# Spreading v over partitions: 10 transfers a tile in place of 16

## The chip, the cores and the metric

The kernel runs on one core of a Trainium2 chip. The metric is the device time of one execution in microseconds (us), the median of several runs. Engines are named as in the profile: PE is TensorE, DVE is VectorE, ACT is ScalarE, POOL is GpSimd, SP is SyncE, which here only issues DMA transfers.

## What is computed

The input x is 2048 tokens by 128 features. A stack of six layers (windowed attention with 16 heads of 64, window 32, then a gated feed-forward part) is run over the normalised input, half of its result is added to x, a Mamba block follows, and the same stack is run once more. What matters here is the attention:

```python
def local_attention(q, k, v):
    b, h, n, d = q.shape
    w = WINDOW                       # 32
    nw = n // w
    bq = q.reshape(b, h, nw, w, d)
    bk = k.reshape(b, h, nw, w, d)
    bv = v.reshape(b, h, nw, w, d)
    def look(t):                     # each window sees itself and the window before
        p = jnp.pad(t, ((0, 0), (0, 0), (1, 0), (0, 0), (0, 0)))
        return jnp.concatenate([p[:, :, :nw], p[:, :, 1:]], axis=3)
    bk2, bv2 = (look(bk), look(bv))
    ...
    out = jnp.einsum('bhwij,bhwje->bhwie', attn, bv2)
for i in range(DEPTH):               # 6
    x = attn_layer(shift_tokens(x), ...) + x
    x = ffn_layer(shift_tokens(x), ...) + x
```

Each window of 32 queries is multiplied with 64 rows of v: the 32 of the window before and its own 32.

## The kernel before

A stack works through N = 96 tiles (16 tiles of 128 tokens, 6 layers), and runs twice. A loop over steps s issues, on each engine, one instruction group of several tiles in an order written out by hand; tile n is projected near step n+18 to n+20 and leaves the attention at step n+23. The engines meet through semaphores alone.

On PE a step is, in this order: scores_high, k_project, out_project (L379), q_transpose (L235), values (L357), k_transpose (L235), in one step of four the feed-forward products (L418 to L420), q_project and v_project (L191 to L193), scores_low (L318 and L296), in one step of four each ffn_centre (L397) and ffn_down (L484), p_transpose (L235) and ffn_variance (L411). The layout of the steps repeats every four tiles, called a cycle here.

The path of v: v_project(n) writes a PSUM slot that q_transpose, v_project and p_transpose take in turns. v_evacuate(n) on ACT (L703) copies it to VT[n % 2], 128 rows (tokens) by 1024 values, and PE's p_transpose(n-1) waits for that copy (L333), because it writes the same slot. SP's spread_values(n) waits for the copy (L1367) and then for values(n-2) (L1371), and issues the transfers that lay v out in V2[n % 2] as four windows of 64 rows for two halves of the heads: destination rows 0 to 63 for one half of the columns, 64 to 127 for the other. Window w holds rows 32w-32 to 32w+31 of the tile; window 0 takes its first 32 rows from the tile before. Each is an SBUF to SBUF DMA of 32 rows of 512 f32 values, that is 64 KB; there are 2 x 4 x 2 = 16 a tile (L1376 and L1378, in turns).

Two waits hold the transfers of a tile n-1 complete: PE's values(n-1) at L344, and ACT's v_evacuate(n) at L700, since the buffer VT[(n-1) % 2] is read by the transfers of two tiles and overwritten by the copy after next. So the copy of tile n starts after all transfers of tile n-1 have landed, and the transfers of tile n start after the copy. ACT works in order: behind v_evacuate stand restore_tables, inverse_norms (L688, L693), carry_evacuate, ffn_square, ffn_rsqrt and p_evacuate (L756).

Of the kernel before, what the change touches and what calls it, by code (L numbers as in the profile page):

```python
# [31 lines left out]
def build(nc, xT, consts, wqkv, wo, w1, w2, lpar, qks, mpar, in_w, xp_w, dt_w, out_w, out):  # L32
    ctx = ExitStack()
    with ctx:
# [3 lines left out]
        def sem(name):  # L38
            return ctx.enter_context(nc.semaphore("s_" + name))
# [27 lines left out]
        def take(n):  # L67
            top[0] += n
            assert top[0] <= 34400, top[0]
            return ARENA[:, top[0] - n:top[0]]  # L70
# [21 lines left out]
        QN, KN, QT, VT = ([take(1024) for _ in range(2)] for _ in range(4))  # L92
# [38 lines left out]
        v2_in = [sem(f"v2_in{i}") for i in range(2)]  # L131
# [34 lines left out]
        def tensor_stack(pe, r):  # L166
            n0, c0, l0 = N * r, 4 * NL * r, NL * r

            def after_tile(eng, sem, n):
                if n >= 0:  # L170
                    eng.wait_ge(sem, n0 + min(n, N - 1) + 1)

            def after_chunk(eng, sem, c):
                if c >= 0:
                    eng.wait_ge(sem, c0 + min(c, N // 4 - 1) + 1)
# [164 lines left out]
            def values(n):  # L340
                if not 0 <= n < N:
                    return
                pe.wait_ge(PT_ev, n0 + n + 1)
                pe.wait_ge(v2_in[n % 2], 256 * ((n0 + n) // 2 + 1))  # L344
                s = n + 22
                after_tile(pe, sub_done, s - 21)
                if s < RAMP or s >= N:
                    after_chunk(pe, f_h[1], (s - 24) // 4 - 1)
                    after_tile(pe, oT_ev, s - 23)
                pt = PTS.rearrange("p (h w x) -> p h w x", h=8, w=4)  # L350
                v2 = V2[n % 2].rearrange("p (w h d) -> p w h d", w=4, h=8)
                for m in range(4):
                    for win in range(4):
                        for side in range(2):
                            hp, col = 2 * m + side, 32 * win
                            out = PS[64 * side:64 * side + 64, 3, 256 * m:256 * m + 256]
                            last = nc.tensor.matmul(  # L357
                                out.rearrange("p (a q) -> p a q", a=2)[:, :, col:col + 32], v2[:, win, hp, :],
                                pt[:, hp, win, :], start=True, stop=True, skip_group_check=True)
                last.then_inc(pv_done, 1)  # L360
# [136 lines left out]
            for s in range(STEPS):  # L497
                scores_high(s - 21)
                k_project(s - 19)
                out_project(s - 23)  # L500
                q_transpose(s - 20)
                values(s - 22)
                k_transpose(s - 20)
                ffn_up0(s - 24)
                ffn_up1(s - 24)
                ffn_up2(s - 24)
                q_project(s - 18)
                v_project(s - 20)
                scores_low(s - 20)
                carry(s - 19)  # L510
                ffn_centre(s - 23)
                ffn_down(s - 24)
                p_transpose(s - 21)
                ffn_variance(s - 23)
# [95 lines left out]
        def scalar_stack(act, r):  # L610
            n0, c0, l0 = N * r, 4 * NL * r, NL * r
# [83 lines left out]
            def v_evacuate(n):  # L695
                if not 0 <= n < N:
                    return
                act.wait_ge(v_done, n0 + n + 1)
                if n:
                    act.wait_ge(v2_in[(n - 1) % 2], 256 * ((n0 + n - 1) // 2 + 1))  # L700
                if n == 1:
                    act.wait_ge(zero_set, r + 1)
                act.activation(VT[n % 2], PS[:, 2, :], ACT.Copy).then_inc(v_ev, 1)  # L703
# [133 lines left out]
            for s in range(STEPS):  # L837
                if s == 19 + 4:
                    high_input(3)
                ffn_high(s - 23)  # L840
                split_k(s - 18)
                exponentials(s - 20)
                q_evacuate(s - 19)
                o_evacuate(s - 21)
                k_evacuate(s - 19)
                gelu0(s - 23)
                gelu1(s - 23)
                gelu2(s - 23)
                q_square(s - 17)
                v_evacuate(s - 19)  # L850
                restore_tables(s - 23)
                inverse_norms(s - 18)
                carry_evacuate(s - 18)
                split_input(s - 24)
                ffn_square(s - 22)
                ffn_rsqrt(s - 22)
                p_evacuate(s - 20)
                k_square(s - 17)
                split_v(s - 19)
                split_q(s - 17)  # L860
# [487 lines left out]
        def sync_stack(sp, r):  # L1348
            n0, c0, l0 = N * r, 4 * NL * r, NL * r

            def load_projection(l):
                for g in range(3):
                    s = slice(1024 * g, 1024 * g + 1024)
                    sp.dma_start(WS[:, s], wqkv[l, :, s]).then_inc(ws_in[g], 16)

            def load_weights(l):
                sp.dma_start(WO[l % 2], wo[l]).then_inc(wo_in[l % 2], 16)
                sp.dma_start(W2[l % 2], w2[l]).then_inc(wo_in[l % 2], 16)

            def load_up(l):  # L1360
                sp.dma_start(W1, w1[l]).then_inc(w1_in, 16)

            def spread_values(n):
                if not 0 <= n < N:
                    return
                v2 = V2[n % 2].rearrange("p (w c) -> p w c", w=4)
                sp.wait_ge(v_ev, n0 + n + 1)  # L1367
                if n == 0:
                    sp.wait_ge(zero_set, r + 1)
                if n >= 2:  # L1370
                    sp.wait_ge(pv_done, n0 + n - 1)  # L1371
                for par in range(2):
                    c = slice(512 * par, 512 * par + 512)
                    for win in range(4):
                        src = VT[n % 2][32 * win:32 * win + 32, c]
                        sp.dma_start(v2[64 * par + 32:64 * par + 64, win, :], src).then_inc(v2_in[n % 2], 16)  # L1376
                        src = VT[n % 2][32 * win - 32:32 * win, c] if win else VT[(n - 1) % 2][96:128, c]
                        sp.dma_start(v2[64 * par:64 * par + 32, win, :], src).then_inc(v2_in[n % 2], 16)  # L1378

            load_projection(0)  # L1380
            load_up(0)
            if r == 0:
                for a, b in ((C[:, 512:1664], consts[:, 512:1664]), (LP, lpar), (QKS, qks), (MP, mpar)):
                    sp.dma_start(a[:, :], b).then_inc(const_in, 16)
            for l in range(2):
                load_weights(l)
            for n in range(N):
                spread_values(n)
                l, T = divmod(n, NT)
                if l + 1 < NL and T == 2:  # L1390
                    for g in range(3):
                        sp.wait_ge(w_lo[g], l0 + l + 1)
                    load_projection(l + 1)
                if l + 1 < NL and T == 12:
                    sp.wait_ge(w1_lo, l0 + l + 1)
                    load_up(l + 1)
                if 1 <= l < NL - 1 and T == 13:
                    sp.wait_ge(f_y, c0 + 4 * l)
                    sp.wait_ge(wo_done, n0 + NT * l)
                    load_weights(l + 1)  # L1400
# [139 lines left out]
```

## Time and profile before

| | |
|---|---|
| median of 3 runs | 3566.99 us (3557.14 to 3574.47) |
| profiled execution | 3554.87 us |
| its span | 3553.0 us |
| granted clock of PE, mean | 0.977 |
| PE busy | 3213.8 us, 90% |
| DVE, ACT, POOL busy | 79%, 71%, 69% |
| DMA q1 (all that SP issues) | 237.59 MB, 27.7% of 16 engines |
| transfers of v | 3072 of 64.0 KB |

The page shows the two stacks (PE at nine tenths) and between them, in a sixth of the span, the Mamba block, in which no v is spread. Times in the views are from the start of the span. An issue row of SP (written SPq) is the time that the queue's instruction took, not the transfer; what was released by a transfer's landing is written as a wait on "DMA ARENA<-ARENA". All large buffers lie in one array, so most rows say ARENA, and the line number tells which step it is.

### The profile page before, as it was taken

Reading aid. Unit: us, or ns where it says so; the run is one execution under the profiler, and the core shown is the slowest. Engines: PE = TensorE matmul, PEld = TensorE weight load, DVE = VectorE, ACT = ScalarE, POOL = GpSimd, SP = SyncE. Lnnn points to the kernel's source line nnn. Section 1 sums busy time; section 2 is a strip of 40 time slices with the busy share of each in tenths; the row PEclk is TensorE's granted clock in tenths of the full one; section 3 lists DMA queues with packets and bytes.
Section 4 is the critical chain, followed back from the end, with each engine's and each line's share of the span. In section 5 each row is a group of like instructions: output and inputs, shape, how many; then the busy total and the mean of one; then the engine's idle time right before and its main releaser. Section 6 shows DMA issues by size and latency. Waiting matters only on the chain. (4 is left out here: it accounts for less than half of the span.)

```text
span 3553.0 us, 121372 instructions
## 1 busy us (share of the span) xinstructions
PE 3213.8 (90%) x51488; PEld 2519.5 (71%) x51488; DVE 2810.5 (79%) x3179; ACT 2508.1 (71%) x3154; POOL 2454.6 (69%) x1241
## 2 busy tenths in 40 slices
PE   6999999999999999986776799999999999999997
PEld 4777777777777777772222677777778778777775
DVE  6787888888788788765886778888888888788884
ACT  4777777777777777766665567777777777777764
POOL 5676776777777677640998667777767668667662
PEclk8999999999999999998999899999999999999999
DMA  3333333233333333221000223333323323323222
GB/s 96 88 75 81 71 82 86 68 79 85 70 79 83 72 75 70 65 61 45 0 0 0 74 68 70 85 73 73 90 66 82 87 66 83 81 68 81 66 63 54
DMA packets 160308, 245.36 MB, mean 69 GB/s; under 512 B 50781, under 2 KB 52638, under 8 KB 159646
## 3 DMA queue, kind: packets, MB, share of 16 engines
q1 hardware_dynamic: 159774, 237.59, 27.7%
q8 instruction: 415, 6.80, 0.8%
q14 instruction: 119, 0.97, 0.1%
HBM read 35.01 MB, written 1.05 MB: 10 GB/s over the span
## 5 line engine op out<-in xcount | busy, mean ns | idle before, releaser
L1269 POOL TENSOR_TENSOR ARENA<-ARENA,RN 128x1024 f32<-128x1024 f32 x192 | 365.3, 1903 | 550.8 <-ACT RN L693 550.7
L235 PE MATMUL PS<-C,ARENA 128*128 128x128 f32 x4608 | 618.5, 278 | 112.5 <-ACT ARENA L703 88.4
L235 PEld LDWEIGHTS PS<-C,ARENA 128*128 128x128 f32 x4608 | 513.0, 141 | 199.1 <-issue 164.0
L1261 POOL TENSOR_TENSOR ARENA<-ARENA 128x1024 f32<-128x1024 f32 x192 | 468.5, 2440 | 264.7 <-DVE ARENA L1002 263.7
L191 PE MATMUL PS<-WL,XH 128*128 128x512 f32 x1152 | 491.1, 426 | 42.4 <-DVE ARENA L987 18.0
L756 ACT ACTIVATE ARENA<-PS 64x1024 f32<-64x1024 f32 x384 | 390.1, 1016 | 111.6 <-PE PS L235 108.2
L1255 POOL TENSOR_TENSOR ARENA<-ARENA 128x1024 f32<-128x1024 f32 x192 | 457.5, 2383 | 8.2 <-DVE ARENA L987 8.1
L357 PE MATMUL PS<-ARENA 128*64 128x64 f32 x12288 | 405.6, 225 | 58.9 <-DVE ARENA L1040 35.4
L193 PE MATMUL PS<-WH,XH 128*128 128x512 f32 x1152 | 457.2, 397 | 0.0
L192 PE MATMUL PS<-WH,XL 128*128 128x512 f32 x1152 | 455.3, 395 | 0.0
L357 PEld LDWEIGHTS PS<-ARENA 128*64 128x64 f32 x12288 | 380.9, 139 | 93.5 <-issue 92.9
L1283 POOL TENSOR_TENSOR ARENA<-ARENA,RI 128x1024 f32<-128x1024 f32 x192 | 365.8, 1905 | 69.6 <-DVE RI L1051 62.9
L980 DVE TENSOR_TENSOR ARENA<-PS,TAB 128x1024 f32<-128x1024 f32 x192 | 235.1, 1225 | 224.5 <-ACT ARENA L675 224.5
L379 PEld LDWEIGHTS PS<-ARENA 128*128 128x128 f32 x3072 | 373.0, 192 | 19.8 <-ACT ARENA L765 2.5
L1032 DVE TENSOR_REDUCE MX<-PS 128x16 f32<-128x1024 f32 x192 | 234.8, 1223 | 189.7 <-PE PS L296 186.5
L379 PE MATMUL PS<-ARENA 128*128 128x128 f32 x3072 | 375.1, 275 | 2.9 <-ACT ARENA L765 2.2
L1277 POOL TENSOR_TENSOR ARENA<-ARENA,RN 128x1024 f32<-128x1024 f32 x192 | 374.6, 1951 | 0.0
L296 PEld LDWEIGHTS PS<-ARENA 64*32 64x32 f32 x24576 | 295.2, 105 | 70.8 <-issue 60.2
L296 PE MATMUL PS<-ARENA 64*32 64x64 f32 x24576 | 329.7, 224 | 0.2 <-issue 0.2
L703 ACT ACTIVATE ARENA<-PS 128x1024 f32<-128x1024 f32 x192 | 196.5, 1024 | 179.7 <-DMA ARENA<-ARENA 142.9
L765 ACT ACTIVATE ARENA<-PS 128x1024 f32<-128x1024 f32 x192 | 197.0, 1026 | 144.5 <-PE PS L357 144.5
L191 PEld LDWEIGHTS PS<-WL,XH 128*128 128x128 f32 x1152 | 218.8, 190 | 103.2 <-issue 40.2
(137 smaller groups left out, 6492.6 us busy)
## 6 DMA issues: line engine op xcount, KB each, us to landing
ARENA<-ARENA SPq DMA_DIRECT2D x3072, 64.0 KB
ARENA<-in_wqkv SPq DMA_DIRECT2D x36, 512.0 KB, 4.9
ARENA<-in_wo SPq DMA_DIRECT2D x12, 512.0 KB, 4.0
ARENA<-in_w SPq DMA_DIRECT2D x12, 341.0 KB, 3.5
ARENA<-in_w SPq DMA_DIRECT2D x12, 192.0 KB, 4.8
X<-in_xT SPq DMA_DIRECT2D x4, 256.0 KB, 5.2
out<-X SPq DMA_DIRECT2D x1, 1024.0 KB, 3.9
QKS<-in_qks SPq DMA_DIRECT2D x1, 768.0 KB, 8.4
```

The lines of the kernel that those rows point to most:

```text
L191: nc.tensor.matmul(o, XH[:, x], WL[:, s], start=True, stop=False)
L192: nc.tensor.matmul(o, XL[:, x], WH[:, s], start=False, stop=False)
L193: last = nc.tensor.matmul(o, XH[:, x], WH[:, s], start=False, stop=True)
L235: last = nc.tensor.transpose(PS[:, slot, 128 * j:128 * j + 128], src[:, 128 * j:128 * j + 128], ident)
L296: last = nc.tensor.matmul(PS[32 * win:32 * win + 32, 3, c:c + 64], q[a:b, hp, 32 * win:32 * win + 32], kt[a:b, hp, 32 * win:32 * win + 64] ...
L357: last = nc.tensor.matmul(out.rearrange("p (a q) -> p a q", a=2)[:, :, col:col + 32], v2[:, win, hp, :], pt[:, hp, win, :], start=True, st ...
L379: last = nc.tensor.matmul(PSB[:, 2, 0:128], w[:, 128 * j:128 * j + 128], OTS[:, 128 * j:128 * j + 128], start=j == 0, stop=j == 7)
L756: last = act.activation(blocks[a:b, :, par, :], PS[a:b, 2, :].rearrange("p (b q) -> p b q", q=32), ACT.Copy)
L1255: nc.gpsimd.tensor_tensor(QN[n % 2], QN[n % 2], T2, ALU.add).then_inc(q_add, 1)
L1261: nc.gpsimd.tensor_tensor(KN[n % 2], KN[n % 2], T2, ALU.add).then_inc(k_add, 1)
L1277: nc.gpsimd.tensor_tensor(a, a, bc(RN[:, n % 2, 16:32], 64), ALU.mult).then_inc(k_nrm, 1)
L1283: nc.gpsimd.tensor_tensor(heads(P), heads(P), bc(RI[:, n % 2, :], 64), ALU.mult).then_inc(p_nrm, 1)
```

## The change

The transfers whose source rows adjoin are joined: for windows 1 to 3 one transfer of 64 rows takes the place of two of 32, and window 0 keeps two of 32 (one from the tile before, one from its own). A tile has 2 x (2 + 3) = 10 transfers, 4 of 64 KB and 6 of 128 KB, with the same bytes to the same places. Each adds 16 to its semaphore, so the two waits count 160 a tile in place of 256.

```diff
@@ values (PE)
-                pe.wait_ge(v2_in[n % 2], 256 * ((n0 + n) // 2 + 1))
+                pe.wait_ge(v2_in[n % 2], 160 * ((n0 + n) // 2 + 1))
@@ v_evacuate (ACT)
-                    act.wait_ge(v2_in[(n - 1) % 2], 256 * ((n0 + n - 1) // 2 + 1))
+                    act.wait_ge(v2_in[(n - 1) % 2], 160 * ((n0 + n - 1) // 2 + 1))
@@ spread_values (SP)
+                last = VT[(n - 1) % 2][96:128, :]
                 for par in range(2):
-                    c = slice(512 * par, 512 * par + 512)
-                    for win in range(4):
-                        src = VT[n % 2][32 * win:32 * win + 32, c]
-                        sp.dma_start(v2[64 * par + 32:64 * par + 64, win, :], src).then_inc(v2_in[n % 2], 16)
-                        src = VT[n % 2][32 * win - 32:32 * win, c] if win else VT[(n - 1) % 2][96:128, c]
-                        sp.dma_start(v2[64 * par:64 * par + 32, win, :], src).then_inc(v2_in[n % 2], 16)
+                    a, c = 64 * par, slice(512 * par, 512 * par + 512)
+                    sp.dma_start(v2[a:a + 32, 0, :], last[:, c]).then_inc(v2_in[n % 2], 16)
+                    sp.dma_start(v2[a + 32:a + 64, 0, :], VT[n % 2][0:32, c]).then_inc(v2_in[n % 2], 16)
+                    for win in range(1, 4):
+                        src = VT[n % 2][32 * win - 32:32 * win + 32, c]
+                        sp.dma_start(v2[a:a + 64, win, :], src).then_inc(v2_in[n % 2], 16)
```

## Rows read from the trace of the kernel before

**Rows 1.** Busy time of all engines in one stretch of 255 us, four cycles:

```profile
core 0: us, PE busy (x) PEld busy (x) DVE busy (x) ACT busy (x) POOL busy (x), PEclk, DMA share, GB/s
567.00:822.00 255.00, 243.95 (x4247) 200.92 (x4245) 210.49 (x242) 190.56 (x237) 183.27 (x92) 0.99 0.33 79
```

**Rows 2.** PE's waits over the span: us in total, times, longest:

```profile
PE PS L235 <- ACT ARENA L703: 88.4, 103, 2.8
...
PE PS L357 <- DVE ARENA L1040: 35.4, 45, 1.3
```

**Rows 3.** ACT's waits over the span, those of v_evacuate:

```profile
ACT ARENA L703 <- DMA ARENA<-ARENA: 142.9, 88, 3.7
...
ACT ARENA L703 <- PE PS L193: 36.8, 104, 1.0
```

**Rows 4.** The line of v_evacuate: count, ns min/median/max, first and last start:

```profile
L703 ACT ACTIVATE ARENA<-PS x192: 1023/1023/1027, 56.0 to 3501.9; 128x1024 f32<-128x1024 f32 x192
```

**Rows 5.** ACT in order of time, seven of the 192 copies of v (L703):

```profile
702.53 1.02 ACT L703 ACTIVATE ARENA<-PS 128x1024 f32<-128x1024 f32 x1 [2.44 <-DMA ARENA<-ARENA]
...
716.91 1.02 ACT L703 ACTIVATE ARENA<-PS 128x1024 f32<-128x1024 f32 x1 [0.35 <-PE PS L193]
...
736.29 1.02 ACT L703 ACTIVATE ARENA<-PS 128x1024 f32<-128x1024 f32 x1 [0.33 <-PE PS L193]
...
752.21 1.03 ACT L703 ACTIVATE ARENA<-PS 128x1024 f32<-128x1024 f32 x1 [0.35 <-PE PS L193]
...
815.84 1.02 ACT L703 ACTIVATE ARENA<-PS 128x1024 f32<-128x1024 f32 x1 [0.35 <-PE PS L193]
829.03 1.02 ACT L703 ACTIVATE ARENA<-PS 128x1024 f32<-128x1024 f32 x1 [0.44 <-DMA ARENA<-ARENA]
844.24 1.02 ACT L703 ACTIVATE ARENA<-PS 128x1024 f32<-128x1024 f32 x1 [2.45 <-DMA ARENA<-ARENA]
```

**Rows 6.** SP's queue in order of time: the transfers of one tile:

```profile
703.58 0.51 SPq L1376 DMA_DIRECT2D ARENA<-ARENA  x1
704.13 0.59 SPq L1378 DMA_DIRECT2D ARENA<-ARENA  x1
704.76 0.59 SPq L1376 DMA_DIRECT2D ARENA<-ARENA  x1
...
707.30 1.45 SPq L1376 DMA_DIRECT2D ARENA<-ARENA  x1
...
713.87 0.59 SPq L1378 DMA_DIRECT2D ARENA<-ARENA  x1
```

**Rows 7.** The chain that ended last, two landings of a tile's last transfer:

```profile
3215.93 3.90 DMA ARENA<-ARENA
...
3413.11 2.04 DMA ARENA<-ARENA
```

**Rows 8.** PE in order of time: transposes after v_evacuate, and values:

```profile
703.70 1.94 PE L235 MATMUL PS<-C,ARENA 128*128 128x128 f32 x8 [2.31 <-ACT ARENA L703]
...
726.23 2.08 PE L357 MATMUL PS<-ARENA 128*64 128x64 f32 x64 [0.38 <-DVE ARENA L1040]
...
789.87 2.08 PE L357 MATMUL PS<-ARENA 128*64 128x64 f32 x64 [1.04 <-DVE ARENA L1040]
...
817.01 1.07 PE L235 MATMUL PS<-C,ARENA 128*128 128x128 f32 x8 [0.21 <-ACT ARENA L703]
```

**Rows 9.** Busy time in stretches of 2 us around the stall at 703:

```profile
702.00:704.00 2.00, 0.30 (x2) 0.33 (x3) 1.60 (x2) 1.35 (x3) 0.00 (x0) 0.84 0.00 0
704.00:706.00 2.00, 2.00 (x41) 1.67 (x39) 0.00 (x0) 0.74 (x3) 1.81 (x1) 0.50 0.28 66
706.00:708.00 2.00, 2.00 (x59) 1.62 (x40) 1.15 (x1) 1.71 (x2) 2.00 (x2) 0.81 0.50 114
```

**Rows 10.** Issue time of a weights load, 128 rows, 512 KB each:

```profile
L1354 SPq DMA_DIRECT2D ARENA<-in_wqkv x36: 328/455/601, 3.1 to 3035.7; - x36
```

**Rows 11.** DVE in order of time, row_max of one step:

```profile
721.68 1.23 DVE L1032 TENSOR_REDUCE MX<-PS 128x16 f32<-128x1024 f32 x1 [1.61 <-PE PS L296]
```

## The prediction

> **What bounds the kernel now.** I read the stretches by engine first. In a stack PE is busy 244 of 255 us, DVE 211, POOL 184 [rows 1]. So PE sets the pace of most steps, and all that a change off PE can win is its idle time, about 11 us in 255, plus what those stalls cost behind them. The list of PE's waits says whose it is: the largest entry is p_transpose (L235) held by the copy of v (L703), 88.4 us in 103 waits; next comes values (L357) held by DVE's subtraction, 35.4 us [rows 2]. The copy of v in turn waits 142.9 us, in 88 of its 192 executions, for transfers to land, and in the other 104 only for the end of v_project, 0.35 us a time [rows 3, 5].
>
> The loop behind it can be timed in one tile. The copy starts at 702.53 and takes 1.02; the first transfer is issued at 703.58, the sixteenth at 713.87, that is 10.29 us for fifteen spacings, fourteen or so of them 0.633 us and one longer because an issue took 1.45 [rows 5, 6]. The last transfer lands 2.04 to 3.90 us after its issue began, mostly near the lower end [rows 7]. Then the next copy may start. The sum is 1.05 + 10.3 + 2.1 = 13.5 us at the least, 15.3 with a late landing.
>
> Against this stands the length of a step when only PE limits it. The starts of the copies give four kinds of step in a cycle. Into the copy at 736.29 (feed-forward products) it is 19.38 us, into that at 752.21 (ffn_down) 15.92, into 829.03, almost without a wait for DMA, 13.19. After a step as short as that the following one is long, 15.21, with 2.45 of waiting [rows 5]. Over all 192 starts [rows 4] the two short kinds last 14.23 us (48 of them) and 14.34 (46) on the mean, and never under 13.12. So the transfer loop binds two steps of four, at 14.3 against 13.15 us, and the two long ones hide it.
>
> **The change, part by part.** *Removed:* six issues a tile. *Added:* nothing on any engine; no wait is new, the two counts only follow the number of transfers. The bytes stay at 1 MB a tile. *Moved:* nothing passes another instruction on SP; the weights loads behind a tile's transfers are issued about 4 us earlier, which nobody waits for.
>
> Nine spacings are left. At the present spacing they are 9 x 0.633 = 5.7 us, with a long issue up to 6.8. The loop becomes 1.05 + 5.7 to 6.8 + 2.1 to 3.9 = 8.9 to 11.8 us. This lies under 13.15 by 1.3 us at the worst, so the loop no longer binds any step.
>
> The price of a 64-row issue is the unknown. The nearest rows are the 32-row issue at 0.59 us [rows 6] and the weights load with 128 rows and eight times the bytes, at 0.455 us [rows 10]. Both say that rows do not cost issue time, so I take 0.6; the ends are 0.45 and, if the cost followed the rows, 1.18. Even at 1.18 (spacing about 1.22) the ten take 4 x 0.633 + 5 x 1.22 = 8.6 us to the last start, and the loop 11.8 with an early landing, 13.6 with a late one: most of the gain would stay.
>
> The moving of the bytes is the other unknown. While 32-row transfers are issued back to back, the DMA engines are busy 0.50 of the time, at 114 GB/s [rows 9]. With 64 rows in the same spacing that doubles to about 1.0 for three transfers running, then falls again. One transfer's own time may so grow by some 0.2 to 0.3 us, which I put on the landing; it is inside the margin above.
>
> A rule of the Trainium skill speaks against the change here (page "SBUF — State Buffer", section "Door 1: The DMA port swizzle"): rows p and p+32 lie on the same port, so 64 rows reach no more ports than 32 do and move no faster in total. By its figures a transfer of 128 KB over eight ports would take about 0.6 us, an estimate, just under the issue spacing; no row of the trace shows it directly.
>
> What goes away on PE:
> 1. The stalls at p_transpose. In steps with neither ffn_centre nor ffn_down (two of four, 96 tiles) only scores_low covers the copy, and 0.21 us remains even when the copy starts at once (the row at 817.01) [rows 8]; in the others nothing remains. 88.4 - 96 x 0.21 = 68 us.
> 2. Part of the stalls at values. A late copy delays all that ACT has behind it in that step, ffn_square among them, and through it DVE's normalisation and subtraction. Where the copy was in time the wait is 0.38 (726.23); where it came late it is 1.04 (789.87) [rows 8]. 35.4 - 46 x 0.38 = 18 us. The ends are 0 and 25.
> 3. The clock behind a long stall. After 2.31 us of idleness the granted clock reads 0.84, 0.50, 0.81 in three stretches of 2 us, that is 3.4 us at 1.2 GHz in place of 2.4, and eight transposes took 1.94 us in place of 1.07 [rows 8, 9]. It costs 1.7 us a time. Of ten full stretches of 255 us five read 0.99 as that of [rows 1] and five 1.00, so I count five or six: 9 us, between 0 and 10.
>
> Sum: 68 + 18 + 9 = 95 us. The starts of the copies give a check: 48 x (14.23 - 13.15) + 46 x (14.34 - 13.19) = 105 us, less 46 x 0.09 because the step into the feed-forward products lasts 19.29 us now and 19.38 where no copy is late: 101 us. I take 97.
>
> What is late next is PE itself. DVE's row_max waits 1.61 us for PE in a step that was not held up [rows 11], so DVE could follow; per cycle (a fourth of 255 us) DVE has 210/4 = 53 us of work and POOL 183/4 = 46 [rows 1], for the 61.6 us that a cycle would last (2 x 13.15 + 15.92 + 19.38).
>
> The profiled execution took 3554.87 us (span 3553.0 and 1.9 around it). 3554.9 - 97 = 3458. It lies 12 us under the median of the runs. If that difference is the scatter of the landings, it disappears with the change and the median is 3458 too; if it is not, the median is 3470. I take the middle, 3464.
>
> **The rivals.**
> - *Another chain takes over (partial gain).* Two short steps in direct succession occur almost nowhere in this trace, since a short one is always followed by a wait for DMA. So the trace cannot show that q's and k's path through the one PSUM slot, ACT, DVE and POOL keeps up for two steps running. For it: DVE is at 83%, and values already waits on it [rows 1, 2]. Against it: the 1.61 us of slack [rows 11]. If the short steps settle at 13.7 us, half of the gain is left: about 48 us, 3512.
> - *The bytes set the spacing (no change).* If a 32-row transfer were issued every 0.633 us because the DMA engines take nothing sooner, a 64-row one would take 1.27, and 4 x 0.633 + 5 x 1.27 = 8.9 us to the last start, which lands 0.6 us later: the 9.5 us of now. Time: 3561. For it: spacing and transfers keep in step, and every issue has the same length. Against it: the engines' share is 0.50 and not 1 [rows 9], and 512 KB were issued in 0.455 us [rows 10]. The Trainium skill leans to this side (page "DMA: Bandwidth & Descriptors", section "Issuing engines are not separate DMA queues"): it calls the time to initiate a transfer "usually small relative to the DMA itself". In this loop 10.3 us of issuing stand against 2.04 of landing, so the trace does not agree.
> - *A 64-row issue costs more than two of 32 (slower).* SP's queue would have to spend over 1.39 us on each (15 x 0.633 = 9.5 = 4 x 0.633 + 5 x 1.39); from there the loop is longer than now. At 1.6 us it is longer by 1.03 us in the 94 short steps, 97 us: about 3658. For it: single issues of 32 rows did take 1.45 us [rows 6]. Against it: these are one in ten or so, the 128-row load [rows 10], and nothing in a joined transfer that the two did not have.
>
> **How the numbers follow.** Forecast (gain 80 to 115 us, 3445 to 3480) 0.76; partial gain (3485 to 3530) 0.12; no change 0.07; slower 0.03; a gain still larger than 115, 0.02. The range from 3445 to 3512 holds the forecast and half or more of the partial case, 0.82 or so. The bound of 0.5% (18 us) is about what a measurement of this kernel can tell from no change. Faster by more: 0.76 + 0.12 + 0.02 = 0.90; within: 0.07; slower: 0.03.
>
> **What would show it.** SP: ten issues a tile of 0.6 us each, the last starting 5.7 to 6.8 us after the first. Landing of the last 2.1 to 2.4 us at best. ACT's wait of L703 on DMA: gone or under 5 us in total. PE's wait of L235 on L703: about 20 us in 100 waits of 0.2. L357 on L1040: about 18 us. The two short kinds of step 13.1 to 13.2 us, the long ones 15.9 and 19.4 as now. PE busy over 0.97 in the stretches of 255 us, with a granted clock of 1.00. I am wrong if the issues of 64 rows are longer than 1.2 us, if the wait on DMA stays above 30 us, or if it is gone and the short steps last over 13.4 us all the same.

## The result

The changed kernel takes 3431.99 us, the median of 4 runs (3429.45 to 3434.12), against 3564.6 (3557.14 to 3574.47) for the kernel before in the same comparison: a ratio of 0.962, 95% interval 0.9596 to 0.9643. That is 132.6 us less, where 100 were forecast (3464, range 3445 to 3512). The direction and the mechanism were right; the size of the gain was forecast too small, and the time lies 13 us under the range. The profiled execution took 3429.45 us, 125.4 less than the profiled one of before.

The page of the changed kernel begins so:

```profile
span 3427.7 us, 120220 instructions
## 1 busy us (share of the span) xinstructions
PE 3186.8 (93%) x51488; PEld 2510.1 (73%) x51488; DVE 2793.1 (81%) x3179; ACT 2511.8 (73%) x3154; POOL 2455.2 (72%) x1241
...
## 4 chain that ended last, share of the span: by engine, by line
PE 37%; DVE 3%; issue 3%; POOL 2%; ACT 2%; POOLq 0%; DVEq 0%; ACTq 0%
```

SP's queue is no longer in the chain that ended last. Next the waits of PE (us in total, times, longest), which answer to [rows 2], and then that of ACT, which answers to [rows 3]:

```profile
PE PS L357 <- DVE ARENA L1040: 25.5, 46, 1.3
...
PE PS L235 <- ACT ARENA L703: 15.9, 81, 0.2
...
PE PS L411 <- ACT ARENA L774: 1.4, 2, 0.7
PE PS L235 <- issue: 1.0, 4, 0.4
```

```profile
ACT ARENA L703 <- PE PS L193: 66.8, 192, 0.9
```

All 192 copies of v now start when v_project ends; none waits for a transfer, where 88 waited 142.9 us in all. The wait of the transposes on the copy went from 88.4 us to 15.9, and is never over 0.2.

The queue of SP in order of time for the ten transfers of one tile in the changed kernel, which answers to [rows 6]:

```profile
688.83 0.54 SPq L1375 DMA_DIRECT2D ARENA<-ARENA  x1
689.41 0.59 SPq L1376 DMA_DIRECT2D ARENA<-ARENA  x1
690.05 1.87 SPq L1379 DMA_DIRECT2D ARENA<-ARENA  x3
691.96 0.59 SPq L1375 DMA_DIRECT2D ARENA<-ARENA  x1
692.60 1.34 SPq L1376 DMA_DIRECT2D ARENA<-ARENA  x1
693.98 1.87 SPq L1379 DMA_DIRECT2D ARENA<-ARENA  x3
```

L1379 is the joined transfer. Its issue times over the run (ns min/median/max):

```profile
L1379 SPq DMA_DIRECT2D ARENA<-ARENA x1152: 472/597/2219, 57.9 to 3386.1; - x192
```

A joined transfer is issued in 0.597 us, the median, against 0.591 for one of 32 rows in the kernel before: twice the rows and bytes, the same price. The starts of the copies on ACT, which answer to [rows 5]:

```profile
687.78 1.03 ACT L703 ACTIVATE ARENA<-PS 128x1024 f32<-128x1024 f32 x1 [0.34 <-PE PS L193]
...
707.15 1.02 ACT L703 ACTIVATE ARENA<-PS 128x1024 f32<-128x1024 f32 x1 [0.33 <-PE PS L193]
...
723.05 1.03 ACT L703 ACTIVATE ARENA<-PS 128x1024 f32<-128x1024 f32 x1 [0.34 <-PE PS L193]
...
736.14 1.02 ACT L703 ACTIVATE ARENA<-PS 128x1024 f32<-128x1024 f32 x1 [0.34 <-PE PS L193]
...
749.25 1.02 ACT L703 ACTIVATE ARENA<-PS 128x1024 f32<-128x1024 f32 x1 [0.35 <-PE PS L193]
```

From copy to copy these steps last 19.37, 15.90, 13.09 and 13.11 us. The two long ones are as they were, and the two short ones follow each other without a wait. In a stretch of 246 us (four of the new cycles) PE is busy 241.31, at the full clock of 2.4 GHz; this answers to [rows 1]:

```profile
2246.00:2492.00 246.00, 241.31 (x4241) 199.41 (x4241) 207.98 (x241) 190.16 (x235) 182.61 (x91) 1.00 0.32 81
```

### The profile page after: what moved, and what is told of

Same layout as the page of the kernel before. It is cut to its first block and busy times, and to the rows that moved or that the text cites. A ratio compares the mean times of both kernels' runs of the same rounds, so it can differ in the third digit from the quotient of the medians.

```text
span 3427.7 us, 120220 instructions
## 1 busy us (share of the span) xinstructions
PE 3186.8 (93%) x51488; PEld 2510.1 (73%) x51488; DVE 2793.1 (81%) x3179; ACT 2511.8 (73%) x3154; POOL 2455.2 (72%) x1241
## 5 line engine op out<-in xcount | busy, mean ns | idle before, releaser
L235 PE MATMUL PS<-C,ARENA 128*128 128x128 f32 x4608 | 613.5, 276 | 32.7 <-ACT ARENA L703 15.9
L235 PEld LDWEIGHTS PS<-C,ARENA 128*128 128x128 f32 x4608 | 512.9, 141 | 110.3 <-issue 73.1
L357 PE MATMUL PS<-ARENA 128*64 128x64 f32 x12288 | 401.7, 224 | 47.3 <-DVE ARENA L1040 25.5
L357 PEld LDWEIGHTS PS<-ARENA 128*64 128x64 f32 x12288 | 377.0, 138 | 82.1 <-issue 81.6
L296 PEld LDWEIGHTS PS<-ARENA 64*32 64x32 f32 x24576 | 292.5, 105 | 69.4 <-issue 59.0
L296 PE MATMUL PS<-ARENA 64*32 64x64 f32 x24576 | 326.3, 223 | 0.0
```

The costliest lines, as they stand in the source:

```text
L235: last = nc.tensor.transpose(PS[:, slot, 128 * j:128 * j + 128], src[:, 128 * j:128 * j + 128], ident)
L296: last = nc.tensor.matmul(PS[32 * win:32 * win + 32, 3, c:c + 64], q[a:b, hp, 32 * win:32 * win + 32], kt[a:b, hp, 32 * win:32 * win + 64] ...
L357: last = nc.tensor.matmul(out.rearrange("p (a q) -> p a q", a=2)[:, :, col:col + 32], v2[:, win, hp, :], pt[:, hp, win, :], start=True, st ...
```

## Experiments

Two theories were to be told apart first. Theory A is the forecast's: only the length of the loop from copy to issues to landing matters, and only where it is longer than a short step. Theory B is that larger transfers help by themselves. Rival C is that each issue saved is worth the same wherever it lies, 22 us.

### The sixteen old transfers, out of the loop

VT has two buffers. The copy of tile n overwrites the buffer that only two of the sixteen transfers of tile n-1 still read, those that take the last rows of the tile before. In this run the two go first, with a semaphore of their own, and the copy waits for them and for the transfers of two tiles ago.

```diff
-                    act.wait_ge(v2_in[(n - 1) % 2], 256 * ((n0 + n - 1) // 2 + 1))
+                    act.wait_ge(last_in[(n - 1) % 2], 32 * ((n0 + n - 1) // 2 + 1))
+                if n >= 2:
+                    act.wait_ge(v2_in[n % 2], 224 * ((n0 + n) // 2))
...
+                for par in range(2):
+                    src = VT[(n - 1) % 2][96:128, 512 * par:512 * par + 512]
+                    sp.dma_start(v2[64 * par:64 * par + 32, 0, :], src).then_inc(last_in[n % 2], 16)
```

> Sixteen transfers of 32 rows as before, but the two that read the tile before go first and have a semaphore of their own; the copy of v waits for these two and for the transfers of two tiles ago, so issuing is off the loop while its count and shape stay. Theory A (only the length of the loop copy, issues, landing matters): as fast as the changed kernel, 3425 to 3440 us, L703 without a wait for DMA. Theory B (larger transfers are themselves what helps, through DMA work or SBUF traffic): near the kernel before, 3550 to 3575 us.

Measured: 3434.38 us (3434.03 to 3438.13), ratio 0.9641 (0.9621 to 0.9661), which the changed kernel's interval overlaps. The copy (here L707) waits for no transfer, and the transposes (here L236) wait as little as in the changed kernel:

```profile
ACT ARENA L707 <- PE PS L194: 67.1, 192, 1.0
```

```profile
PE PS L236 <- ACT ARENA L707: 15.6, 80, 0.2
```

So the gain is not in the shape of the transfers or in their number. It comes from taking the issues out of the wait: making fewer of them does it, and so does waiting for fewer. Theory B falls.

### The dose: 13, 14, 15 and 18 transfers

In these runs some windows use the joined transfer and the others the two old ones; for 18, two of the old ones are cut into 16 rows each.

```diff
+                        if (par, win) in joined:
+                            src = VT[n % 2][32 * win - 32:32 * win + 32, c]
+                            sp.dma_start(v2[a:a + 64, win, :], src).then_inc(v2_in[n % 2], 16)
+                            continue
```

> Thirteen transfers a tile: one half of the columns in joined transfers (5), the other in the old ones (8). Theory A (threshold): the loop is 14.3 - 3 x 0.633 = 12.4 us on the mean, under the 13.1 us of a short step, so nearly all of the gain: 3430 to 3445 us. Rival C (each issue taken away is worth the same, 132.6/6 = 22 us): 3564.6 - 66 = 3498 us.

> Fourteen transfers a tile (two pairs joined), the edge of the threshold. Theory A: mean loop 14.3 - 2 x 0.633 = 13.0 us against 13.1 of a short step; only tiles with a late landing or a long issue pay, some 10 to 20 us over the changed kernel: 3442 to 3455 us. Rival C (equal worth of each issue): 3564.6 - 44 = 3520 us.

> Fifteen transfers a tile (one pair joined). Theory A: loop 14.3 - 0.63 = 13.7 us, 0.57 us over the short step in place of 1.2, so about half of the cost is left: 3432 + 60 = 3492 us (3475 to 3510). Rival C: 3564.6 - 22 = 3543 us.

> Eighteen transfers a tile (two of the old ones cut into 16 rows each). Theory A: loop 14.3 + 1.27 = 15.6 us, 2.5 us over each of the two short steps in 48 cycles, 240 us over the changed kernel: 3672 us (3650 to 3700; more if the 15.9 us step is caught too). Rival C: 3564.6 + 44 = 3609 us.

| transfers a tile | us, median (range) | ratio to before, 95% interval | waits of the copy on DMA, us (times) |
|---|---|---|---|
| 10 (changed kernel) | 3432.0 (3429.5 to 3434.1) | 0.9596 to 0.9643 | 0 |
| 13 | 3435.4 (3429.8 to 3437.4) | 0.9611 to 0.9661 | 4.9 (5) |
| 14 | 3442.1 (3439.1 to 3451.0) | 0.9632 to 0.9669 | 22.9 (27) |
| 15 | 3485.5 (3475.5 to 3497.5) | 0.9753 to 0.9814 | 72.9 (59) |
| 16 (kernel before) | 3566.5 (3556.1 to 3573.3) | | 142.9 (88) |
| 18 | 3700.5 (3693.9 to 3706.3) | 1.0358 to 1.0412 | 233.4 (92) |

The last column comes from these rows, of the runs with 13, 14, 15 and 18 transfers in turn:

```profile
ACT ARENA L703 <- DMA ARENA<-ARENA: 4.9, 5, 2.0
```

```profile
ACT ARENA L703 <- DMA ARENA<-ARENA: 22.9, 27, 2.2
```

```profile
ACT ARENA L703 <- DMA ARENA<-ARENA: 72.9, 59, 2.4
```

```profile
ACT ARENA L703 <- DMA ARENA<-ARENA: 233.4, 92, 4.6
```

The profiled executions with 14 and with 15 transfers are the slowest of their four, so their waits stand for the upper end. It is a threshold. The first issue taken away (16 to 15) is worth 81 us, the next 43, the next 7, and the last three together 3; the last two of these differences are not clear of the noise, since the intervals of the ratios overlap. Rival C, at 22 us each, misses every run by 57 to 91 us. The edge lies where theory A put it, at 14 transfers. With 18 it was 28 us too low, just beyond its own bound; the two steps grew to 15.80 and 15.50 us, worked out from the start times of the copies, and the clock took more too (a mean of 0.961).

### One late copy in a cycle

To find what a late copy costs in each kind of step, the changed kernel got eighteen transfers in one tile of four. In the run at0 the copy of the first short step is late, in at1 that of the second, where ffn_centre also stands between v_project and the transposes.

```diff
+                        cuts = (0, 64) if n % 4 != 0 else (0, 16, 32, 64) if win == 1 else (0, 32, 64)
+                        for i, j in zip(cuts, cuts[1:]):
+                            src = VT[n % 2][32 * win - 32 + i:32 * win - 32 + j, c]
+                            sp.dma_start(v2[a + i:a + j, win, :], src).then_inc(v2_in[n % 2], 16)
```

> The changed kernel with eighteen transfers in tiles 0, 4, 8, ... alone, so that only the copy of v in the first short step of a cycle (nothing but scores_low covers it) is late, by 15.65 - 13.1 = 2.55 us. Both theories: 48 x 2.55 = 122 us over the changed kernel, about 3554 us. It is the measure for the run at1.

> The same with eighteen transfers in tiles 1, 5, 9, ..., so that only the copy of the second short step is late by 2.55 us, where ffn_centre too stands between v_project and the transposes. Theory D (as forecast): ffn_centre covers up to 0.97 us of it, and values pays 0.66 more: 48 x (2.55 - 0.97 + 0.66) = 108 us at the most, 76 without the share of values: 3508 to 3540 us. Theory E: the lateness is paid in full, since ffn_square, behind the copy on ACT, is late too and holds ffn_variance, and through the normalisation values: 48 x 2.55 = 122 us or more, 3554 us and up, with waits of L411 on L774 and larger gaps before L357.

Measured: at0 3624.9 us (3617.9 to 3629.0), at1 3598.3 us (3584.3 to 3605.1). At0 is 71 us over what both theories gave, at1 beyond the range of theory D and above the floor of E. Both are slower than the kernel before (ratios 1.0156, 1.0138 to 1.0174; 1.0076, 1.0054 to 1.0098), though only one tile of four has the long transfers. The copies (here L706) waited for DMA 148.2 us in at0 and 161.4 in at1, in 48 each; less the 0.35 us that a copy always waits, they were late by 2.74 and 3.01 us, 0.2 and 0.5 more than assumed. The cost was 192.9/48 = 4.02 us a cycle in at0 and 166.3/48 = 3.46 in at1, more than the lateness. PE in order of time and in stretches of 4 us, in at0:

```profile
787.23 1.94 PE L238 MATMUL PS<-C,ARENA 128*128 128x128 f32 x8 [4.18 <-ACT ARENA L706]
```

```profile
782.00:786.00 4.00, 1.05 (x73) 0.83 (x72) 3.25 (x3) 0.00 (x0) 0.79 (x1) 1.00 0.61 152
786.00:790.00 4.00, 2.77 (x71) 2.47 (x72) 0.00 (x0) 2.56 (x5) 2.28 (x2) 0.53 0.26 59
790.00:794.00 4.00, 4.00 (x36) 3.25 (x20) 2.45 (x2) 2.02 (x3) 3.80 (x2) 0.61 0.69 172
```

PE stands still for 4.18 us, and the granted clock (the column PEclk) then reads 0.53 and 0.61: 1.2 GHz for most of the 8 us behind the stall. The same stands in [rows 9] behind a shorter stall. The mean granted clock of at0 is 0.958, of at1 0.965, of the changed kernel 0.980. What this cost can be read from PE's busy time, since its work is the same: 3251.4 us in at0 and 3250.2 in at1 against 3186.8, so 65 and 63 us more.

The other part is idle time at the transposes behind the late copy (here L238), in at0 and then in at1. Some of it is put down to "issue"; by their times the long ones of these too stand behind the late copies:

```profile
PE PS L238 <- ACT ARENA L706: 139.2, 81, 4.4
PE PS L238 <- issue: 8.3, 4, 4.6
```

```profile
PE PS L238 <- ACT ARENA L706: 87.9, 115, 4.2
PE PS L238 <- issue: 32.8, 17, 3.9
```

Less the 15.9 and 1.0 us of the changed kernel, that is 130.6 us more in at0 and 103.8 in at1, for a lateness of 48 x 2.74 = 132 and 48 x 3.01 = 144 us. So the lateness is paid in full where nothing but scores_low covers it, and ffn_centre covers 41 us of it in at1, 0.85 us a time, where theory D allowed up to 0.97. Idle and busy time together make up 195 of the 199.5 us by which the span of at0 is longer, and 167 of the 172.8 of at1. Neither theory is borne out in its total, since both left out the clock. One part of theory E is shown, though. PE's wait of ffn_variance (here L414) for ffn_square is 7.1 us in at1,

```profile
PE PS L414 <- ACT ARENA L777: 7.1, 31, 0.7
```

and 1.4 in at0 and in the changed kernel. ffn_square stands behind the copy on ACT, so a late copy in that step holds it. That makes 5.7 us more of the 172.8. The other part, that values then waits longer for DVE's subtraction, is not shown: that wait is 23.0 us in at1, 32.0 in at0 and 25.5 in the changed kernel.

### Towards a faster kernel: v first

What L235 still waits for in the changed kernel is the copy, never over 0.2 us at a time. In this run v_project goes ahead of q_project in the three steps of four without feed-forward products, and the copy ahead of q_square on ACT.

```diff
-                q_project(s - 18)
-                v_project(s - 20)
+                if s % 4 == 3:
+                    q_project(s - 18)
+                    v_project(s - 20)
+                else:
+                    v_project(s - 20)
+                    q_project(s - 18)
```

> The changed kernel with v_project ahead of q_project in the steps without feed-forward products, and with the copy of v ahead of q_square on ACT. The copy then has 1.4 us more cover, so the 15.9 us of waits of L235 on L703 go: 3414 to 3420 us. If the later q_project holds k_project in the next step (through q_square and DVE's two rotations, which had about 1.9 us of slack), it is the same or slower: 3432 us and up, with new waits of L191 on L987.

Measured: 3486.13 us (3483.39 to 3490.01), ratio 0.977 (0.9755 to 0.9786), 54 us slower than the changed kernel. The rival's row is there, k_project waiting for the rotation of q:

```profile
PE PS L191 <- DVE ARENA L995: 86.9, 102, 7.6
```

In the changed kernel it is

```profile
PE PS L191 <- DVE ARENA L987: 18.6, 6, 7.6
```

q's path had less slack than the 1.9 us that I had taken. In the changed kernel the rotation of q (L987) ends 0.9 us before k_project starts, the median in both kinds of short step. In the kernel before it is 0.9 us in the first and 2.1 in the second, whose start lies behind a stall of PE: that stall was part of the slack. Laying q_project 1.4 us later, with q_square behind the copy on ACT too, was more than the 0.9 could bear, and k_project waits some 0.7 us in each of the 96 short steps.

### Towards a faster kernel: cutting the scores elsewhere

The scores of a tile are computed in two halves of four pairs of heads, before and after the transposes of P. Moving one or two pairs to the first half lays more work beside the copy.

```diff
-                score_tiles(n, range(4))
+                score_tiles(n, range(6))
...
-                score_tiles(n, range(4, 8)).then_inc(S_done, 1)
+                score_tiles(n, range(6, 8)).then_inc(S_done, 1)
```

> The changed kernel with the scores cut 5 and 3 pairs of heads in place of 4 and 4 between scores_low (ahead of the transposes of P) and scores_high (behind them). It lays 0.2 us more matmuls beside the copy of v, what L235 still waits for L703 in two steps of four (15.9 us in 81 waits). Theory F: these waits go and nothing else moves: 3432 - 16 = 3416 us (3414 to 3422). Rival G: DVE is next, and L357 waits longer for L1040: 3425 to 3433 us.

> The same with 6 and 2 pairs. Theory F: no more than 5 and 3, since the wait is gone there: 3414 to 3422 us. Rival G: as the run before, 3425 to 3433 us. A change in the clock or in row_max, which now starts 0.4 us sooner behind the transposes, would show here and not there.

Measured: 5 and 3 pairs 3424.29 us (3419.06 to 3425.91), ratio 0.9598 (0.958 to 0.9615), an interval that overlaps that of the changed kernel, though the times themselves do not; 6 and 2 pairs 3406.87 us (3404.78 to 3408.45), ratio 0.9551 (0.9535 to 0.9568), clear of it. The wait of L235 on L703 is gone in both, so neither theory explains why the first pair gave 8 us and not 16, and the second 17 us more. PE in order of time, the groups of scores of one step, in the changed kernel, then with 5 and 3 and with 6 and 2 pairs:

```profile
736.26 0.84 PE L296 MATMUL PS<-ARENA 64*32 64x64 f32 x64
738.30 0.86 PE L296 MATMUL PS<-ARENA 64*32 64x64 f32 x64
```

```profile
736.34 1.01 PE L296 MATMUL PS<-ARENA 64*32 64x64 f32 x80
738.39 0.72 PE L296 MATMUL PS<-ARENA 64*32 64x64 f32 x48
```

```profile
729.57 1.15 PE L296 MATMUL PS<-ARENA 64*32 64x64 f32 x96
731.67 0.46 PE L296 MATMUL PS<-ARENA 64*32 64x64 f32 x32
```

The two groups take 1.70, 1.73 and 1.61 us. Over the whole run PE is busy on L296 for 326.3 us in the changed kernel, 332.9 with 5 and 3 pairs and 310.2 with 6 and 2. So with 5 and 3 the same matmuls take 6.6 us longer, which is most of the 8 that are missing. With 6 and 2 they take 22.7 us less than that, of which values gives back some 6: its wait on L1040 goes from 24.8 to 31.0 us, as rival G has it. Why a second group of 32 matmuls takes less than its share was not tried.

## Why the prediction was right and where it was too small

The mechanism held, and the size failed. The steps of the prediction that were wrong are terms of its sum: the clock, put at 9 us, where PE's busy time fell by 27.0 (13 of it by the mean granted clock, the rest with an open cause); the stalls at p_transpose, put at 68 us, where 80.8 went; and ffn_variance behind the late copy, put at nothing, where 6.9 went. A gain over 115 us, which is what came, had been given a chance of 0.02.

**The bound.** Right. The loop over two short steps of four was the cost, and PE was next.

**The spacing and the price of a 64-row issue.** Right: 0.6 was taken, 0.597 measured; the last of ten issues starts 6.5 us after the first, the median of the 192 tiles (5.7 to 6.8 was the forecast). The highest that was read while joined transfers are issued is a DMA share of 0.82 at 201 GB/s, in a stretch of 1.6 us, against 0.50 and 114 in [rows 9]; the stretches of 2 us from 690 and from 692 read 136 and 164 GB/s:

```profile
691.40:693.00 1.60, 1.60 (x68) 1.28 (x68) 0.46 (x1) 1.32 (x3) 1.60 (x1) 1.00 0.82 201
```

So the rival in which the bytes set the spacing is gone. The sentence that the prediction set beside it says that the time to initiate a transfer is usually small relative to the transfer (Trainium skill, "DMA: Bandwidth & Descriptors", section "Issuing engines are not separate DMA queues"). It speaks of one transfer, and for one, 0.59 us of issuing stands beside 2.04 from the issue to the landing, which neither bears it out nor contradicts it. The 10.3 us that the prediction set against the 2.04 are sixteen issues in a row, against the landing of one. The port rule (Trainium skill, "SBUF — State Buffer", section "Door 1: The DMA port swizzle") held no issue back: its estimate of 0.6 us for 128 KB lies just under the spacing of the issues, 0.64 us. No row shows how long one joined transfer itself takes, nor when the last of a tile lands, so neither the rule nor the forecast of 2.1 to 2.4 us for the landing is tested; that the whole loop is shorter than a short step is shown by the waits that are gone.

**The rival of another chain** did not come: two short steps run back to back at 13.1 us, where it had 13.7.

**The sum.** By its terms, against the span and the waits of the two profiles:

| term | forecast, us | measured, us |
|---|---|---|
| p_transpose | 68 | 72.5 on L703 and 8.3 on "issue", 80.8 |
| ffn_variance (L411) | 0 | 8.3 - 1.4 = 6.9 |
| values (L357) | 18 | 35.4 - 25.5 = 9.9, and 1.5 on "issue" |
| PE's busy time | 9, as clock | 3213.8 - 3186.8 = 27.0 |
| all | 95 | 126 (span: 125.3) |

The two rows of before that the forecast did not use are these, from the list of PE's waits:

```profile
PE PS L235 <- issue: 9.3, 12, 2.4
PE PS L411 <- ACT ARENA L774: 8.3, 37, 0.7
```

1. *p_transpose*: I left out the part that the profile puts down to "issue", and took off 96 times 0.21 where 15.9 us remained.
2. *ffn_variance*: the prediction says that a late copy delays "all that ACT has behind it in that step, ffn_square among them", and costs only the effect on values. The run at1 shows the term: 7.1 us of it with late copies in that step, 1.4 without.
3. *values*: this term was too large, 18 us where 9.9 to 11.4 went. The floor of 0.38 us was read in a cycle whose other short step was late; that DVE had had time to catch up there is my reading. With both in time the mean is 25.5/46 = 0.55 us; one row of the changed kernel:

```profile
697.10 2.08 PE L357 MATMUL PS<-ARENA 128*64 128x64 f32 x64 [0.45 <-DVE ARENA L1040]
```

4. *busy time*: this is the largest miss, 18 us. The forecast counted stalls from stretches whose clock is printed with two digits. The mean granted clock went from 0.977 to 0.980; 0.023 x 3553 - 0.020 x 3428 = 13 us, against the 9 allowed. The other 14 us lie inside rows that count as busy. The page says that the ends of matmuls are modelled, so a stall begins, in the rows, only behind the modelled end of the group before, and its first part is booked as work. That this is where they lie is my reading, not shown by a run, and at0 speaks against it: there the idle time alone, 130.6 us, is the whole lateness of 132. The cause of the 14 us stays open.

**The check by start times** was the better sum, 101, and it too was low, since I took its floors (13.15, 13.19) from steps that were themselves a little late. Worked out in the same way from the start times of after, the short steps last 13.10 and 13.03: 48 x 1.13 + 46 x 1.31 = 114.5 us. The step into the feed-forward products did not grow by 0.09 (19.27 us), the fourth kind gave 44 x 0.10 = 4, and the first and last steps of the two stacks, which I had left out, some 6.

**The median.** Of the two readings of the 12 us between profile and median I took the middle. The runs settle it: the kernel before ranges over 17 us, the changed one over 4.7, and the one with sixteen transfers out of the loop over 4.1. The scatter was that of the landings and went with the loop. The median should have been taken at the profile's sum, 3458. That is 6 of the 32 us between 3464 and 3432. The sum is 28 of them (125.4 where 97 was taken), and 2.5 go the other way, since the median of the changed kernel lies that much above its profiled execution.

**The range** reached down only to a gain of 120 us, while the text had itself set PE's idle time at 11 of 255 us and added the clock. Every term that I left at zero or put at its row's face could only raise the gain, so the lower end needed more room than 19 us.

## What to carry to other kernels

A chain that binds only some steps costs next to nothing up to the length of a free step and its excess beyond, and more than that where the stall brings the clock down, so find that length first. Before making transfers fewer, see which of them the wait is for: here two of sixteen, and issuing these first, with a semaphore for them alone, gave the same gain. To size a stall that goes away, use the distance between starts of the same instruction in free and in held-up steps, over all steps; the row of one wait leaves out what is booked as "issue", the slower work behind the stall, and what the same late instruction holds further down its own engine.

## What the runs showed of the hardware

- Issue time on SP's queue does not follow the rows: 0.591 us for 32 rows of 2 KB, 0.597 for 64.
- A long stall of PE costs more than its length. In at0, with one late copy in four tiles, PE stands still 131 us longer than in the changed kernel, and its own work, which is the same, takes 65 us longer; behind a stall of 4.18 us the granted clock reads 0.53 and 0.61. In the kernel before, with shorter stalls in two steps of four, it is 81 and 27 us, and the mean clock is 0.977 against 0.958. So at0 is slower than the kernel before, though only one tile of four has long transfers.
- Cutting the same 128 small matmuls of a tile 96 and 32 in place of 64 and 64 shortens them from 326.3 to 310.2 us over the run, and 80 and 48 lengthens them to 332.9. The first makes the fastest kernel here, 3406.87 us; the cause is open.
